# A hybrid attention and expert layer: the second FFN in two passes of slots, the causal mask on VectorE, and seven places for expert weights

## What is computed

```python
x = x + attn_a(layernorm(x))    # 16 heads of 8, log-sparse mask
x = x + ffn(layernorm(x))       # 8 experts, one per token (argmax of 8 affinities)
x = x + attn_b(layernorm(x))    # 16 heads of 64, causal mask, softmax over 256 keys
x = x + ffn(layernorm(x))       # the same experts again
```

## Time and profile before

| | us |
|---|---|
| median of 3 runs (lowest, highest) | 559.36 (557.67, 563.07) |
| the profiled execution | 564.56 |
| its span, first to last instruction | 562.8 |
| PE busy in the span | 462.9 (82%) |
| DVE busy | 373.5 (66%) |
| ACT busy | 229.0 (41%) |
| POOL busy | 236.3 (42%) |

### The profile page before, as it was taken

The page is one execution under the profiler, slowest core; times in us unless marked ns, Lnnn a source line. Parts: engine busy times, 40 slices in busy tenths (PEclk is TensorE's granted clock), DMA queues, the critical chain, the costliest instruction groups (busy, mean ns, idle before and its releaser), DMA issues.

```text
span 562.8 us, 10440 instructions
## 1 busy us (share of the span) xinstructions
PE 462.9 (82%) x3500; PEld 363.3 (65%) x3500; DVE 373.5 (66%) x1093; ACT 229.0 (41%) x835; POOL 236.3 (42%) x247
## 2 busy tenths in 40 slices
PE   3957994705989399999999999999999996429893
PEld 2324563605988257787877878777787875329893
DVE  6599976852656279767589585985858762345662
ACT  2620001502534035555466563674645742105441
POOL 5002884471444235524335334562445534123443
PEclk9979998555999689999999999999999997659998
DMA  8999600034464200000000000000000000034560
GB/s 310 403 421 422 269 1 1 24 107 140 132 180 146 78 1 1 2 2 1 1 0 4 0 1 11 20 11 1 2 11 20 12 1 28 10 111 152 160 190 5
DMA packets 21942, 47.73 MB, mean 85 GB/s; under 512 B 3297, under 2 KB 13544, under 8 KB 19458
## 3 DMA queue, kind: packets, MB, share of 16 engines
q1 hardware_dynamic: 18882, 40.73, 20.9%
q0 software_dynamic: 3008, 6.34, 3.3%
HBM read 23.82 MB, written 24.15 MB: 85 GB/s over the span
## 4 chain that ended last, share of the span: by engine, by line
PE 68%; DVE 9%; POOL 9%; DMA 6%; issue 5%; ACT 1%; SPq 0%; POOLq 0%; ACTq 0%; DVEq 0%
PE ps L895 10%; PE ps L924 8%; PE ps L971 8%; PE ps L958 7%; PE ps L840 7%; PE ps L853 6%; PE ps L912 6%; PE ps L902 5%; POOL sum L443 4%; PE ps L930 3%; DMA pv<-in_w 3%; POOL sum L447 2%; PE ps L688 2%; POOL sorted_in L468 2%; PE ps L794 1%
## 5 line engine op out<-in xcount | busy, mean ns | idle before, releaser
L498 POOL TENSOR_TENSOR vT<-vT,prec 128x256 f32<-128x256 f32 (+1 forms) x128 | 103.0, 825 | 145.9 <-DVE prec L1386 145.9
L639 ACT ACTIVATE vT<-ps,nmax 128x128 f32<-128x128 f32 (+1 forms) x256 | 104.9, 433 | 21.1 <-DVE nmax L1378 21.1
L647 ACT COPY prod<-ps 128x384 f32<-128x384 f32 x96 | 42.9, 481 | 111.4 <-PE ps L958 108.3
L1378 DVE TENSOR_REDUCE nmax<-ps 128x2 f32<-128x256 f32 (+1 forms) x128 | 62.3, 550 | 22.4 <-PE ps L930 22.4
L895 PE MATMUL ps<-xnT,wb 128*128 128x256 f32 x256 | 68.0, 389 | 1.7 <-DVE qk L1363 1.2
L958 PEld LDWEIGHTS ps<-cst,vT 128*128 128x128 f32 x384 | 44.8, 141 | 18.8 <-issue 14.0
L639 ACT ACTIVATION_READ_ACCUMULATOR vT<-ps,nmax 128x1 f32 x256 | 56.0, 219 | 0.0
L958 PE MATMUL ps<-cst,vT 128*128 128x128 f32 x384 | 52.8, 274 | 1.8 <-POOL vT L498 1.7
L853 PE MATMUL ps<-w2s,pv 128*128 (+1 forms) x368 | 49.8, 279 | 2.6 <-issue 2.6
L971 PE MATMUL ps<-prod 128*64 128x256 f32 (+1 forms) x512 | 50.0, 339 | 1.4 <-ACT prod L647 1.4
L924 PE MATMUL ps<-qk 64*128 64x128 f32 (+1 forms) x512 | 51.1, 338 | 0.0
(11 more groups left out here) (152 smaller groups left out, 831.4 us busy)
## 6 DMA issues: line engine op xcount, KB each, us to landing
sorted_in<-zero SPq DMA_DIRECT2D x1, 16512.0 KB, 58.9
pv<-in_w SPq DMA_DIRECT2D x30, 259.0 KB, 2.9
pv<-sorted_in SPq DMA_DIRECT2D x46, 129.0 KB, 2.7
wps<-in_w SPq DMA_DIRECT2D x1, 2072.0 KB, 8.5
w2s<-in_w SPq DMA_DIRECT2D x1, 2048.0 KB, 12.9
wb<-in_w_b SPq DMA_DIRECT2D x1, 1536.0 KB, 17.3
xres<-in_x SPq DMA_DIRECT2D x4, 256.0 KB, 3.6
b2s<-in_b SPq DMA_DIRECT2D x1, 512.0 KB, 14.3
```

The lines of the kernel that those rows point to most:

```text
L498: last = nc.gpsimd.tensor_tensor(px, px, view(prec, m_at(n, x) + t * 2, [[1, 2], [0, (t + 1) * P]]), ALU.mult)
L639: last = nc.scalar.activation(pb[:, o:o + (t + 1) * P], wide[:, c:c + (t + 1) * P], ACT.Exp, bias=nmax[:, m:m + 1], accum_out=psum[:, m:m ...
L647: nc.scalar.copy(pT[:, c:c + BLOCKS * P], bank[hh][:, 0:BLOCKS * P]).then_inc(b_pa, 1)
L1378: last = nc.vector.tensor_reduce(nmax[:, m:m + 2], view(wide, x * 1024 + t * P, [[512, 2], [1, (t + 1) * P]]), AX.X, ALU.max, negate=True)
```

## The change

1. **Mask.** `mask_b` is gone from PE. DVE adds the mask itself, in the instruction that also finds the maximum: `tensor_tensor_reduce` computes (score + mask) times -1 in place in PSUM and the minimum over the row. It works on one head and one row tile, so there are eight per step in place of four reductions. The mask tile is a float32 one in SBUF, with 128 zero columns in front for the rows that see a full block. ACT exponentiates with scale -1. `scores_b` gives one signal per step, behind both pairs, in place of one per pair behind each mask.
2. **Copy of v.** It moves from DVE to ACT, between the third copy of weights and the second pair's exponentials.
3. **Group work in the steps.** `count`, `rank` and `place` of groups 0 to 2 come a step earlier, and so do their dispatches.
4. **Two passes.** The second expert block has its own tables for groups 0 to 2 (19 slots, 8 static and 11 dynamic) and for group 3 (11 slots, 8 and 3), which it runs one behind the other as 30 slots. Group 3's preparation, and both sets of tables, stand between the slots of the first pass. To make room in PSUM, the transposed input and the output have one place each in this block in place of two (`depth`).
5. **Seven weight places** (`WR = 7`), each freed when the hidden layer of its slot is through relu, no longer when its output is done. This holds for the first expert block too.

The core of the diff:

```diff
-NSLOT = (NTOK + NE * (P - 1)) // P
-NDYN = NSLOT - NE
+PASS = ((0, 1, 2, 3), (0, 1, 2), (3,))
+PTOK = tuple(len(g) * GT * P for g in PASS)
+NSLOT = tuple((n + NE * (P - 1)) // P for n in PTOK)
+NDYN = tuple(n - NE for n in NSLOT)
+RUN = ((S0[0], S0[1]), (S0[1], S0[3]))
-XR, WR, YR = 8, 4, 4
+XR, WR, YR = 8, 7, 4
...
 # SyncE, slots(q)
                 def load_w(d):
-                    need(sp, f_y, k * NSLOT + (NE + d - WR + 1 if d >= WR else 0))
+                    before = [m for m in range(S0[3]) if slot(m)[1] >= NE and dyn(m) == D0[q] + d - WR]
+                    need(sp, f_ha, before[0] + 1 if before else 0)
+                    need(sp, f_hv, before[0] + 1 if before else 0)
...
+            slots(2)
...
 # POOL
-            dispatch(1, NG - 2)
+            dispatch(1, NG - 2, range(1, GT))
             powers(1, NG - 1)
-            dispatch(1, NG - 1)
-            for s in range(NSLOT):
-                give_back(1, s, out.rearrange("b l d -> (b l) d"))
+            for m in range(*RUN[1]):
+                give_back(m, out.rearrange("b l d -> (b l) d"))
+                i = m - S0[1] - 9
+                if 0 <= i < GT:
+                    if i == 0:
+                        pool.wait_ge(f_sent, (2 * NT - GT) * 16)
+                    dispatch(1, NG - 1, [i])
...
 # ACT, step
                 if ok(n):
                     copy_p(n, 1, 1)
+                if some(bv) and j != 1 or some(b) and j == 1:
+                    copy_v(n, (j + 2) % STEPS)
                 if ok(n1):
                     exp_b(n1, 1)
...
 # ACT, ffn(k)
+                    if k == 1 and m - lo == 4:
+                        turned_v(1, NG - 1)
+                    if k == 1 and m - lo == 6:
+                        residual(1, NG - 1)
+                    if k == 1 and m - lo == 8:
+                        exps(1, NG - 1)
...
 # PE, ffn(k)
+                    if k == 1 and m - lo == 5:
+                        turn_v(1, NG - 1)
+                    if k == 1 and m - lo == 7:
+                        affinity(1, NG - 1)
+                    if k == 1 and m - lo == 10:
+                        rank(1, NG - 1)
+                        totals(2)
...
+            def depth(m):
+                return 2 if slot(m)[0] == 0 else 1
 # PE: turn_x waits for f_xs, output for f_ys, each m + 1 - depth(m)
...
 # PE, step
                 if ok(n1):
                     scores_b(n1, 0)
                     scores_b(n1, 1)
-                    mask_b(0)
                 if ok(n):
                     turn_p(n, 0)
-                if ok(n1):
-                    mask_b(1)
...
 # DVE
+            def max_b(n, x, hh, t):
+                m, c, open_at = m_at(n, x) + t * 2 + hh, (2 * x + hh) * 512 + t * P, C_CAUSAL - t * P
+                s = wide[:, c:c + (t + 1) * P]
+                ins = nc.vector.tensor_tensor_reduce(out=s, in0=s, in1=cst[:, open_at:C_CAUSAL + P], scale=-1.0,
+                                                     scalar=-MASKED * 2, op0=ALU.add, op1=ALU.min,
+                                                     accum_out=nmax[:, m:m + 1])
+                if hh and t:
+                    ins.then_inc(b_mx, 1)
...
 # DVE, ffn(k)
+                    if k == 1 and m - lo == 0:
+                        spread(NG - 1)
+                    if k == 1 and m - lo == 1:
+                        tables(1)
+                    if k == 1 and m - lo == 2:
+                        norm(1, NG - 1)
+                    if k == 1 and m - lo == 7:
+                        choose(1, NG - 1)
+                    if k == 1 and m - lo == 8:
+                        count(1, NG - 1)
+                    if k == 1 and m - lo == 10:
+                        place(1, NG - 1)
+                        take_totals(2)
+                    if k == 1 and m - lo == 13:
+                        tables(2)
```

More of the change, by code:

```diff
@@ L72 @@
 C_REGION = C_PART + 1
[L73 removed]
+C_COLS = C_REGION + 2 * GT * NE
 def constants():
@@ L282, in wait_all, with slot, dyn, landed @@
-        def wait_all(eng, sem_list, k, total):
-            for i, sm in enumerate(sem_list):
-                eng.wait_ge(sm, landed(k + 1, i, len(sem_list), total))
-        def w1_of(s):
-            return (wps, s * WP) if s < NE else (wring[(s - NE) % WR], 0)
+        def slot(m):
+            q = sum(m >= S0[i] for i in (1, 2))
+            return q, m - S0[q]
+        def dyn(m):
+            q, s = slot(m)
+            return D0[q] + s - NE
+        def landed(i, ring):
+            return 16 * (i // ring)
@@ new lines, in turn_x, with hidden @@
+            def turn_x(m):
+                pe.wait_ge(f_ld[m % XR], landed(m, XR) + 16)
+                need(pe, f_xs, m + 1 - depth(m))
+                nc.tensor.transpose(turned_ps(m)[:, 0:P], xs[m % XR][:, 0:D], ident).then_inc(f_tx, 1)
+            def hidden(m):
+                tile, b = w1_of(m)
+                pe.wait_ge(f_xs, m + 1)
+                need(pe, f_ha, m - 1)
+                need(pe, f_hv, m - 1)
+                for c in range(FC):
+                    last = nc.tensor.matmul((hid_act, hid_dve)[c // 2](m)[:, c % 2 * P:(c % 2 + 1) * P],
+                                            tile[:, b + c * P:b + (c + 1) * P], xsT[m % 2][:], start=True, stop=True)
+                last.then_inc(f_h, 1)
@@ new lines, in output @@
+            def output(m, at_e):
+                s = slot(m)[1]
+                pe.wait_ge(f_ha, m + 1)
+                pe.wait_ge(f_hv, m + 1)
+                need(pe, f_ys, m + 1 - depth(m))
+                for c in range(FC):
+                    w = w2s[:, s * F + c * D:s * F + (c + 1) * D] if s < NE else \
+                        w2s[:, bass.ds(at_e[s - NE] + c * D, D)]
+                    last = nc.tensor.matmul(y_ps(m), hT[m % 2][:, c * P:(c + 1) * P], w, start=c == 0, stop=c == FC - 1)
+                last.then_inc(f_y, 1)
@@ L1444, in _ @@
             means(1, NG - 1)
-            spread(NG - 1)
-            norm(1, NG - 1)
-            choose(1, NG - 1)
-            count(1, NG - 1)
-            place(1, NG - 1)
-            tables(1)
             ffn(1)
```

459 lines of the change are left out of this document (220 added, 239 removed).

## The result

The median rose from 559.55 us (20 runs, 556.85 to 563.09) to 563.56 us (20 runs, 560.79 to 565.52): ratio 1.0064, 95% interval 1.0045 to 1.0083. A second series (e12) gave 1.0089, 1.0056 to 1.0122. The change made the kernel slower, by 3.6 to 5 us. That is less than the 1% of the prediction's bound, but the intervals exclude no change, and 555.2 was forecast: the sign was wrong.

The account below looks back on a forecast made before the run. PE was taken to bound the attention, mostly the ring of four results the second block's slots. Attention -3.5, weight places -2 and second block +1.3 sum to -4.2: median 559.36 becomes 555.2 us, range 545 to 569.

Parts of the forecast that it names:

- Sum 7.51. So a plain step costs 7.5: Attention: the loop from scores through maxima, exponentials and copies to values sets a plain step at 7.5 us, before 7.41.
- I take -3.5 us for the attention: Attention: PE time saved in steps with other work, against some 20 plain steps at +0.1, nets -3.5 us.
- I take -2: First expert block: seven weight places cut ACT's 7.4 us of waits for weights, saving 2 us.
- The bound I had named: First expert block: the seven weight places might gain 0, at the other end 4 us.
- Together +1.3: Second expert block: 74.9 us in place of 72.6, so +2.3, less 1 for transfers, makes it 1.3 us slower.
- 59.2 + 9.6 - 1 = 67.8: Second expert block: 29 slot periods of 2.04 us, 9.6 us of inserted work left unhidden, 1 us off for transfers.
- the -1 for transfers that collide less: Second expert block: 14 weights over 70 us instead of 15 over 50 collide less, saving 1 us.
- 0.7 of a period is free, and seven slots with insertions hide 5 of the 15: Second expert block: DVE's free 0.7 us per slot hides 5 of 15 us of inserted work, leaving about 10.
- the writes catch up behind the tables: Second expert block: while PE waits behind the second slot's tables, the write of results catches up; no separate size given.
- The insertions cost in full: Rival, second expert block: none of the 15 us is hidden and half clock returns, +5 to +7, so 561; chance 0.15.
- The maxima are dear: Rival, attention: a pair's maxima hold DVE 1.9 us or more rather than 1.46; 563 to 568 us; chance 0.25.
- the 570: Attention: by the skill page's rule, without overlap on DVE, maxima take 2.1 us, a step 8.15, the total 570.

Follow-up runs that it names:

- e12: The changed kernel, unchanged, run again for a second profile: 563.67 us, ratio 1.0089 to the kernel before.
- e5: e1 with ACT's copy of v and last copy of weights moved between the first pair's two exponentials: 554.15 us, ratio 0.9909 to the kernel before.
- e2: The changed kernel with group 3's tables, tables(1), moved in two pieces to DVE in the attention's last two steps: 559.01 us, ratio 1.0003 to the kernel before.
- e7: e2 with the second set of tables, tables(2), cut into eight pieces behind slots 13 to 20: 561.20 us, ratio 1.0063 to the kernel before.
- e9: e8 with tables(1) cut into pieces for the gaps of the attention's last two steps: 552.55 us, ratio 0.9876 to the kernel before.
- e10: e9 with norm of group 3 spread over three slots and the pieces of tables(2) one slot later: 555.25 us, ratio 0.9919 to the kernel before.
- e11: e7 with the pieces of tables(2) one slot later, behind slots 14 to 21: 555.78 us, ratio 0.9926 to the kernel before.
- e8: e7 with e5's order of copies added: 557.85 us, ratio 0.9976 to the kernel before.
- e3: The changed kernel with four weight places in place of seven: 561.31 us, ratio 1.0036 to the kernel before.
- e4: The changed kernel with the copy of v back on DVE, ahead of the second pair's maxima: 578.97 us, ratio 1.0315 to the kernel before.
- e1: The kernel before with only parts 1 to 3 of the change, one pass and four weight places: 553.53 us, ratio 0.9869 to the kernel before.

## Why the prediction was wrong

- **"Sum 7.51. So a plain step costs 7.5": the loop was right, its size a little too long.** It closes through the engines named, and PE waits where I said. It takes 7.38: maxima 1.37 from the first one's start to the first exponential (forecast 1.58, because I let each reading of a result hold DVE for 0.09, and it holds nothing), inversion and signal 0.21 (0.29), and against that 0.87 from the copy of v to the values (0.66). e5 shows it is the bound: with the copies moved, the step falls to 7.03.
- **"I take -3.5 us for the attention": too small, by 1.7 us or more.** The means of the profiles give -7.4: six sequences gained 4.6, the last steps 1.0, the first lost 0.5, and 2.2 is an output projection that ran at full clock in both profiles of after and at half in both of before. That last term I had not thought of, and it is not the mask's; without it the gain is 5.2. Nor did after keep it: the first slot's rows had not landed, and PE waited 1.7 us for them. From the start of the last output projection to the first finish it took 11.4 and 10.2 us in after, and 10.5 to 10.7 in e2, e7, e9, e10 and e11, where the projection ran at half clock. (In e8 it took 8.4, with the full clock and the rows already there.) The low clock did not stay away either. It fell elsewhere: on the first slots in after and e3 (1.53 for the first hidden layer of after), and a step earlier in e12 and e4. Why it falls where it does is open. e1's -7.3 by the median is near the -7.4 partly by chance, since its own last output projection ran at half clock.
- **"I take -2" for seven places: 0.** The bound I had named came true. ACT's waits for weights went, and DVE waits longer for the ring of four results; e3, with four places, has 4.7 us of waits for weights again and is no slower.
- **The second block, "Together +1.3": this step failed.** It cost 7.1 by the profiles, perhaps more by the medians. Of the 5.8 above the forecast, 3.7 lie in the slots, about 1.2 in the start (6.1; measured 7.6 and 6.3 to the start of the first finish), and 0.9 in the block of before, which the second profile has shorter. The slots with insertions were to take 59.2 + 9.6 - 1 = 67.8 and took 71.4 and 71.7. No run isolates the -1 for transfers that collide less. The error is in "0.7 of a period is free, and seven slots with insertions hide 5 of the 15". A slack of 0.7 us hides a piece of 0.7 us, not its share of a piece of 4.3. Behind each set of tables PE waited 3 us, and then ran a slot or so at half clock, which I had given to a rival only. I had also reckoned that the writes catch up behind the tables; there was little to catch up on, since slots without inserted work run at 1.90, near the 1.89 that PE alone needs.
- **The rival "The insertions cost in full" is what happened**, in its mechanism: little or nothing hidden, and the half clock behind the tables. By its terms the block takes 6.1 + 59.2 + 15 - 1 = 79.3 us to the last finish's end, and took 79.3 and 78.4. That its time (561) is near the median is partly luck: it kept my -3.5 and -2, which erred in opposite directions, and the profiles do not place the last 3.6 us. e2, e9 and e11 show it by removing the cause: first to last finish falls from 71.4 to 66.1 with tables(1) away, and to 63.2 to 64.0 with tables(2) in pieces too, so the tables cost 7.4 to 8.2 us there. For the rest of the inserted work, the preparation of group 3, nothing was removed. "The maxima are dear" fell, and with it the 570: 453 and 306 ns, and only steps of the first sequence lost more than 0.05 us (the worst 8.70 in place of 7.67).
- **Two passes in themselves.** With the tables out of the way the block takes 67.6 us from the end of the attention to the last finish (e9; before 72.3 and 70.5), 3 to 5 us less there. Against e5, which has the same attention and one pass, it is 3.0 less in the block (70.7), of which the attention's last steps, with tables(1) in them, give 0.8 back. By medians two passes are not shown to beat one: with e5's order of copies e9 has 0.9876 (0.9833 to 0.9919) and e5 0.9909, without it e11 0.9926 and e1 0.9869. The mask with the group work (e1) is as fast as any of them within the intervals.

## What to carry to other kernels

Where an engine has slack in every period, compare each inserted piece with the slack of one period, not the sum of pieces with the sum of slacks; a longer piece stops the neighbour, and on PE the stop was paid twice here, in the wait and in the clock after it. Before placing such work, look for a gap as long as the piece (in after DVE had 2.65, 1.66 and 3.93 us idle just ahead of the block), and cut the work to the gaps; e10 shows that the consumer's fixed place limits how far a cut may reach. Measure the parts of a change apart: one part here was worth 7 us and was hidden by another. And add up neighbouring stages before calling a gain in one of them a gain: the 2.2 us of the last output projection went into a wait for rows just behind it.

## What the runs showed of the hardware

- The reading of an accumulator on DVE shows 140 ns and costs none: in after the next main instruction starts at the same time (as at 291.00) behind 195 of the 256 readings.
- PE's clock fell to half behind waits of 3.21 and 3.01 us in after and 2.82 in e10. It also fell near the end of the attention, or just behind it, in every profile, at places that differ: in e9 at about 462, where the longest wait just before was 1.78, while after has the same wait of 1.78 and kept the full clock.
- Some very short DVE instructions stretched while POOL divided. In e2 the one on 128x8 from 464.07 took 0.91 us, with POOL's division running from 463.34 to 464.95; in after the same instruction (L1298 at 482.68) took 0.17, with no division running. e9 has 0.91 again (460.74, division from 460.01 to 461.62). The one that reduces 128x88 at 463.43 in e2 kept its 0.24. The Trainium skill says that the Pool engine shares a read and a write interface with DVE, and that this conflicts with DVE instructions in a 2-port mode or with two inputs in SBUF ("Advanced Engine Details and Errata", Miscellaneous Facts); the rows agree with sharing but don't isolate it, and no row shows the mode.
- In e7 and e8, at the same two slots, ACT and DVE waited some 3 us for signals of PE matmuls that had ended by the records. e11 and e9 differ from them by a few moved DVE instructions, in e11 all behind the first of the two places, and have no such wait. So at least for the first place it isn't the order of the work; where the code stands in memory is a guess that I did not test. It cost e7 about 4 us (68.25 against 63.95), as much as what was being measured.
